# Turning the attention probabilities by DMA, as pairs of half floats

## What is computed

```python
q = rope(x @ wq.T + bq)      # 16 heads of 128
k = rope(x @ wk.T + bk)
v = x @ wv.T + bv
attn = einsum('bihd,bjhd->bhij', q, k) / sqrt(128)
attn = softmax(where(causal, -inf, attn))
o = einsum('bhij,bjhd->bihd', attn, v)
out = o @ wo.T + bo + residual
# beside it: 32 experts (top 4 of them for each token) and a shared expert
```

## Time and profile before

| | |
|---|---|
| median of 3 runs | 1025.46 us (1025.29 to 1025.47) |
| the profiled execution's own time | 1025.06 us |
| its span | 1023.3 us |
| PE busy | 1011.4 us, 99% |
| DVE busy | 711.6 us, 70% |
| ACT busy | 664.6 us, 65% |
| POOL busy | 774.1 us, 76% |
| granted TensorE clock | 1.00 of full speed over the span |

### The profile page before, as it was taken

One profiled execution on the slowest core, in us unless ns is written; L12 is line 12 of the kernel. 1 busy time (PEld: TensorE's weight loads), 2 busy tenths in 40 slices (PEclk: granted clock), 3 DMA queues, 4 the chain that ended last, 5 costly groups with the idle time before them and its releaser, 6 DMA issues.

```text
span 1023.3 us, 18770 instructions
## 1 busy us (share of the span) xinstructions
PE 1011.4 (99%) x6461; PEld 906.3 (89%) x6461; DVE 711.6 (70%) x1745; ACT 664.6 (65%) x1454; POOL 774.1 (76%) x660
## 2 busy tenths in 40 slices
PE   8999999999999999999999999999999999999998
PEld 4887898999989898989899899899998989898997
DVE  8757778787787888766666656666666566665676
ACT  5677666666667767665766656666566666656664
POOL 4879886758687786768786776978867879687866
PEclk9999999999999999999999999999999999999999
DMA  7222426212121212322232223333224232322232
GB/s 249 65 62 52 124 57 130 48 32 47 42 62 38 47 42 62 48 52 74 73 102 77 59 70 84 91 85 77 63 68 103 67 86 54 82 69 66 48 106 83
DMA packets 51694, 75.42 MB, mean 74 GB/s; under 512 B 12304, under 2 KB 29072, under 8 KB 51472
## 3 DMA queue, kind: packets, MB, share of 16 engines
q1 hardware_dynamic: 45920, 67.40, 25.2%
q0 software_dynamic: 5392, 6.56, 4.2%
q10 hardware_dynamic: 288, 0.26, 0.1%
HBM read 33.94 MB, written 10.90 MB: 44 GB/s over the span
## 4 chain that ended last, share of the span: by engine, by line
PE 93%; DVE 3%; POOL 1%; ACT 1%; DMA 1%; issue 0%; SPq 0%; DVEq 0%; POOLq 0%; ACTq 0%
PE ps L302 25%; PE ps L304 25%; PE ps L303 25%; PE ps L441 12%; PE ps L531 3%; PE ps L543 1%; DVE st L1238 1%; DVE ps L1552 0%; ACT prob L1044 0%; PE ps L517 0%; DMA xt<-x 0%; DVE xn L1264 0%; DVE acc L1599 0%; POOL qb L1705 0%; POOL qb L1701 0%
## 5 line engine op out<-in xcount | busy, mean ns | idle before, releaser
L1701 POOL TENSOR_TENSOR qb<-qb,k_sb 128x512 f32<-128x512 f32 x128 | 172.1, 1344 | 141.8 <-DMA qs<-qb 141.4
L1552 DVE CUSTOM_DVE_ANT_0 ps<-ps,maskr 128x128 f32<-128x128 f32 (+7 forms) x256 | 193.6, 762 | 57.4 <-PE ps L304 57.2
L1044 ACT ACTIVATE prob<-ps,nmax 128x128 f32<-128x128 f32 (+7 forms) x256 | 190.6, 744 | 60.7 <-DVE nmax L1552 59.1
L1055 ACT ACTIVATE ptd_h<-ps 128x128 fp32r<-128x128 f32 (+3 forms) x256 | 109.4, 436 | 147.3 <-PE ps L441 146.4
L1562 DVE TENSOR_TENSOR ptd_l<-ps,ptd_h 128x128 fp32r<-128x128 f32 (+3 forms) x256 | 124.4, 486 | 81.1 <-ACT ptd_h L1055 78.8
L1705 POOL TENSOR_TENSOR qb<-qb,qs 128x512 f32<-128x512 f32 x128 | 165.1, 1290 | 18.4
L441 PE MATMUL ps<-k_sb,prob 128*128 128x128 f32 x1152 | 172.7, 274 | 3.0 <-ACT prob L1044 1.5
L1702 POOL TENSOR_TENSOR qs<-qs,k_sb 128x512 f32<-128x512 f32 x128 | 172.5, 1348 | 0.0
L441 PEld LDWEIGHTS ps<-k_sb,prob 128*128 128x128 f32 x1152 | 135.2, 141 | 20.0 <-ACT prob L1044 2.6
L302 PE MATMUL ps<-k_h,q_h 128*128 128x512 f32 (+3 forms) x384 | 140.1, 365 | 0.0
L1599 DVE SCALAR_TENSOR_TENSOR acc<-ps,rinv,acc 128x256 f32<-128x256 f32 x256 | 111.4, 477 | 32.3 <-PE ps L304 30.8
(11 more groups left out here) (193 smaller groups left out, 2627.6 us busy)
## 6 DMA issues: line engine op xcount, KB each, us to landing
qs<-qb SPq DMA_DIRECT2D x256, 128.0 KB
ew<-epack SPq DMA_DIRECT2D x16, 768.0 KB, 4.2
rqk<-wqk SPq DMA_DIRECT2D x16, 256.0 KB, 3.0
rv<-wvp SPq DMA_DIRECT2D x8, 256.0 KB, 3.1
ro<-wop SPq DMA_DIRECT2D x16, 128.0 KB, 2.3
token_table<-xn SPq DMA_DIRECT2D x4, 512.0 KB, 5.1
token_sum<-token_table SPq DMA_DIRECT2D x1, 2048.0 KB, 9.3
token_sum<-x POOLq DMA_DIRECT2D x1, 2048.0 KB, 16.7
```

The source lines that it names most:

```text
L1044: act.activation(prob[:, t % 2, 0:w], tile[t], ACT.Exp, bias=nmax[:, t:t + 1], scale=-1.0, accum_out=rsum[:, t:t + 1]).then_inc(exp_done, 1)
L1055: act.activation(turned(0, t, j0, w), src, ACT.Copy).then_inc(pth_done, 1)
L1552: dve.tensor_tensor_reduce(out=tile[t], in0=tile[t], in1=maskr[:, SEQ - w:SEQ], scale=-1.0, scalar=3e38, op0=ALU.add, op1=ALU.min, accum_o ...
L1701: pool.tensor_tensor(qb[:, i, :], qb[:, i, :], cos_sb[:, c], ALU.mult).then_inc(rope_a, 1)
```

## The change

Transposes, and the copies out of PSUM behind them, go. `exps` writes the exponentials back into the tile's own place in PSUM. `prob_hi` on ACT scales them by 2^15 and writes them as a half float (float16) to `halves`, and `prob_lo` on DVE subtracts that from the scaled value and writes the rest as a second half float. `turn` is now a list entry of SP: for each tile two transposing DMAs (`dma_start_transpose`, the high and the low part, each of 128 x (t + 1) 128 elements of two bytes) from `halves` to `pt`, that is 16 DMAs in a unit. The four buffers of `halves` go by t mod 4, and `prob_hi` waits on `turned` of the tile four before it. `scores` waits on `lo_done` of the tile that was in its place, where it waited on `exp_done`.

`weighted` takes `pt` and the values, which are now split into half floats too, and has the same 36 matmuls. So that the values fit, `v_hi` and `v_lo` scale them by a power of two that the kernel works out for each pair of heads (`features`, `value_parts`, `value_scale` on DVE and `bound` on PE, once in four units), and `out_hi` and `out_lo` undo both scales (`oscale`).

```diff
-            def turn(n, g):
-                t, j0, w = TGROUPS[g]
-                pe.wait_ge(exp_done, TILES * n + t + 1)
-                bank = take("T", n, g)
-                for j in range(w):
-                    ins = pe.transpose(bank[:, j * P:(j + 1) * P], prob[:, t % 2, (j0 + j) * P:(j0 + j + 1) * P], ident)
-                ins.then_inc(t_done, 1)
...
-                    pe.wait_ge(exp_done, TILES * n + {0: -1, 2: 0, 4: 2, 5: 4, 6: 5, 7: 6}[t])
+                    pe.wait_ge(lo_done, TILES * n + {0: -1, 2: 0, 4: 2, 5: 4, 6: 5, 7: 6}[t])
...
+            def weighted(u, c):
+                for b in range(GT):
+                    pe.wait_ge(turned[b], 32 * (2 * u + c + 1))
+                pe.wait_ge(vl_done, 4 * (u // 2) + (2, 4)[c])
+                bank = take("PV", u, c)
+                d = slice(u % 2 * DK, (u % 2 + 1) * DK)
+                for j in range(4 * c + 4):
+                    a = max(0, j - 4 * c)
+                    ins = three(pe, bank[:, a * P:CH].rearrange("p (a b) -> p a b", b=P), (v_h[:, j, d], v_l[:, j, d]),
+                                [pt[c][i][:, a:GT, j, :] for i in range(2)], j == 0, j == 4 * c + 3)
...
+        def turn(sp, n, t):
+            if n and t % GT == 0:
+                sp.wait_ge(pv_done, 2 * (n - 1) + t // GT + 1)
+            for i, done in enumerate((hi_done, lo_done)):
+                sp.wait_ge(done, TILES * n + t + 1)
+                sp.dma_start_transpose(pt[t // GT][i][:, t % GT, 0:t + 1, :],
+                                       halves[t % GT][:, i, 0:(t + 1) * P]).then_inc(turned[t % GT], 16)
...
+                act.activation(tile[t], tile[t], ACT.Exp, bias=nmax[:, t:t + 1], scale=-1.0,
                                accum_out=rsum[:, t:t + 1]).then_inc(exp_done, 1)
...
+            def prob_hi(n, t):
+                act.wait_ge(exp_done, TILES * n + t + 1)
+                if n or t >= GT:
+                    act.wait_ge(turned[t % GT], 32 * (2 * n + t // GT))
+                act.activation(halves[t % GT][:, 0, 0:(t + 1) * P], tile[t], ACT.Copy, scale=PSCALE).then_inc(hi_done, 1)
...
+            def prob_lo(n, t):
+                dve.wait_ge(hi_done, TILES * n + t + 1)
+                h = halves[t % GT]
+                dve.scalar_tensor_tensor(out=h[:, 1, 0:(t + 1) * P], in0=tile[t], scalar=PSCALE, in1=h[:, 0, 0:(t + 1) * P],
+                                         op0=ALU.mult, op1=ALU.subtract).then_inc(lo_done, 1)
...
+            def value_parts(g):
+                scaled(dve.tensor_reduce(vpart[:, :], w, AX.X, ALU.max))
+                scaled(dve.tensor_reduce(vleast[:, :], w, AX.X, ALU.min))
+                scaled(dve.scalar_tensor_tensor(out=vpart[:, :], in0=vleast[:, :], scalar=-1.0, in1=vpart[:, :],
+                                                op0=ALU.mult, op1=ALU.max))
+                dve.tensor_tensor(vpart[:, :], vpart[:, :], xmax[:, :], ALU.mult).then_inc(vpart_done, 1)
```

More of the change, by code:

```diff
@@ L55 @@
 MASKS = 9
-TGROUPS = [(t, j, min(4, t + 1 - j)) for t in range(TILES) for j in range(0, t + 1, 4)]
-NTG = len(TGROUPS)
+PSCALE = 2.0 ** 15
+VTOP = 2.0 ** 14
 def batch_of(n):
@@ L478, in weighted_part @@
                 for j in range(last + 1):
-                    o = slice((2 * h + (j == last)) * P, (2 * h + 2) * P)
-                    if j < 4:
-                        pt = [ptr[i][:, j, o] for i in range(2)]
-                    else:
-                        pt = [ptd[i][:, j - 4, P + o.start:P + o.stop] for i in range(2)]
-                    ins = three(pe, bank[:, o], (v_h[:, j, d], v_l[:, j, d]), pt, j == 0, j == last)
+                    a = 2 * h + (j == last)
+                    ins = three(pe, bank[:, a * P:(2 * h + 2) * P].rearrange("p (a b) -> p a b", b=P),
+                                (v_h[:, j, d], v_l[:, j, d]), [pt[1][i][:, a:2 * h + 2, j, :] for i in range(2)],
+                                j == 0, j == last)
                 ins.then_inc(pv_done, 1)
@@ L586, in _ @@
             gate_turn(0)
+            bound(0)
             turn_x(2, 0)
@@ L674, in _ @@
                 masks(n, 3)
[L675 to L677 removed]
+                if n % 4 == 3:
+                    bound(n // 4 + 1)
+                weighted(n, 0)
             u = UNITS - 1
[L680 to L684 removed]
             outproj(u, 0, 0)
             outproj(u, 0, 1)
+            weighted_part(u, 0)
             weighted_part(u, 1)
@@ L780, in _ @@
                 g = n // 4
+                turn(sp, n - 1, 7)
                 load_ew(sp, n)
                 swap(sp, n + 1, 1)
+                for t in range(4):
+                    turn(sp, n, t)
                 swap(sp, n + 1, 2)
+                turn(sp, n, 4)
                 swap(sp, n + 1, 3)
+                turn(sp, n, 5)
                 if n == 1:
@@ L1065, in out_hi_part @@
                 o = slice(2 * h * P, (2 * h + 2) * P)
-                act.activation(oh[1][:, o], rbank("PW" if h else "PV", u, 1)[:, o], ACT.Copy).then_inc(oh_done, 1)
+                g = u // 4 % 2
+                act.activation(oh[1][:, o], rbank("PW" if h else "PV", u, 1)[:, o], ACT.Copy,
+                               scale=oscale[:, g:g + 1]).then_inc(oh_done, 1)
             def expert_tanh(n):
@@ L1330, in _ @@
             x_lo(1, 1)
+            dve.memset(sums[:, :], 1.0)
+            features()
+            value_parts(0)
             stats(2, 1)
@@ L1645, in _ @@
                 route(n, 0)
-                turned_lo(n, 1)
-                recips(n - 1, 1)
                 expert_copy(n)
-                turned_lo(n, 2)
+                prob_lo(n, 2)
+                prob_lo(n, 3)
                 recips(n, 0)
-                out_lo(n - 1, 1)
-                maxes(n, 4)
                 route(n, 1)
-                turned_lo(n, 3)
                 if n % 4 == 2 and g < PAIRS - 1:
@@ L1663, in _ @@
                     wo_lo(dve, 2 * g + 1)
+                maxes(n, 4)
+                if n % 4 == 3 and g < PAIRS - 1:
+                    value_parts(g + 1)
+                    wv_lo(dve, g + 1)
+                prob_lo(n, 4)
+                out_lo(n - 1, 1)
                 maxes(n, 5)
+                route(n, 2)
+                prob_lo(n, 5)
+                maxes(n, 6)
                 add_out(n - 1, 1, 0)
-                maxes(n, 6)
-                turned_lo(n, 4)
                 add_out(n - 1, 1, 1)
```

245 lines of the change are left out of this document (114 added, 131 removed).

## The result

The changed kernel takes 1084.02 us (median of 3 runs, 1083.92 to 1090.2) against 1025.46: ratio 1.059, interval 1.0535 to 1.0648. It is slower by 59 us, where the forecast of 918 us was faster by 107: a miss of 166 us, and outside the range. The median is one of three runs that lie 6.3 us apart, so that differences from it of that size are not clear of noise.

A forecast was written before the change was run, and what follows sets the result against it. PE, busy 99%, was taken as the bound. Savings of 15 x (4.7 - 1.4) and 16 x (4.7 - 0.7) us, with 6 added, took 107.5 off 1023.3; with 1.8 around the span, 918 us, range 880 to 1,035.

The forecast's parts named there:

- The waits this makes: Walk through two plain units' lists: PE loses 1.4 us a plain unit; 0.7 us taken with expert work.
- ACT and DVE: Same 36 blocks in 8 operations each in place of 12; some 17 us of 25 busy, costing latency, not throughput.
- POOL behind the swaps: POOL's waits for swaps queued behind turns on SP: 2.7 us of room in expert units, costed at nothing.
- the ring: Named after the run: mask, exponential, high, low, next mask; one tile at a time round DVE and ACT.
- POOL bound: Rival: swaps come 1 to 3 us later behind the turns, expert units go by POOL; 934 to 958 us, chance 0.07.
- The issue price: SP's time to issue a DMA, 0.47 or 0.60 us; sixteen make 8.5 us a unit, hidden.
- SP's cover: SP's issuing stays hidden in a 25 us unit until an issue takes 1.3 us.
- The rival on the slower side: Transposes' throughput: tiles go out in small pieces, PE waits at both weighted sums; 1,200 or 2,000 us, chance 0.20.
- The clock: PE's granted clock, taken as 1.00; a fall in PE's new gaps would show the forecast wrong.
- Tile 7's landing: Its turned low part lands 2.3 us after issue, covered by 0.6 us before weighted(n-1, 1), the thinnest cover.
- the swap loop: Named after the run: projection copy, swap's place in SP's list, landing, three POOL operations, `rope_hi` on ACT.
- C, the banks held longer: Theory of the experiments: a tile keeps its PSUM banks for four steps in place of two, and scores wait.

The follow-up runs named there:

- e1_merged: Changed kernel with one transposing DMA for both parts of a tile, 8 in a unit in place of 16, same bytes: 1106.0 us.
- e2_one_block: Changed kernel with the sixteen DMAs turning only the first block of each tile, which the weighted sum takes for all blocks: 1072.1 us.
- e18_early_ahead_late: Changed kernel with swap 2 behind turn 1, mask passes ahead of low parts (tiles 4 to 7), `rope_hi` behind high part 4: 1043.3 us.

## Why the prediction was wrong

**The step that failed** is "The waits this makes", with the sentence under ACT and DVE that leads to it: "Neither comes near its unit: some 17 us of 25. Here the change does not cost throughput, it costs latency." Its verdict is true: neither engine is full, and the cost is latency. Its size is not: DVE is busy 671.7 / 31 = 21.7 us a unit and ACT 18.9, where the earlier trace rows already had 20.7 and 18.6 in a plain unit. And I priced the latency only at the places of my walk, around tile 7 and at the unit's end, as 1.4 us and 0.7 us a unit, with nothing at tiles 4 to 6 and nothing for `rope_hi`. Measured, PE is idle for 4.5 us a unit and loses 1.8 more with it, 6.3 in all. I never followed the four steps of one tile into the mask of the next as a loop of its own. In unit 17 the four tiles' steps from mask 4 (612.29) to the exponential of tile 7 (629.21) take 17 us, in which DVE sits idle for 4.39 + 2.34 + 0.52 = 7.3 us and ACT for some 9.

**"POOL behind the swaps ... I cost them at nothing"** failed with it, and made it worse. POOL had the room that I gave it (22.7 us busy of 31), but its output stands in ACT's list ahead of high parts, so POOL's lateness is paid in the ring: ACT waited 66.9 us for it, where it waited 9.5. I asked whether POOL would be full, and not who waits for it. The rival "POOL bound" had swaps 1 to 3 us late; swap 2 left a median 7.1 us behind its copy, and swap 1, which left on time, landed 1.6 us later than before. With each loop in place, removing the other gives 2 or 3%; the sum over both is 100 us.

**The issue price.** 0.47 or 0.60 us was taken for an issue, 1.27 came. My own threshold of 1.3 us (SP's cover) was nearly reached: 16 x 1.27 + 4.3 = 24.6 us. It was not the bound, since the unit went to 31 us (e1_merged). But four tiles' turnings hold SP for 10 us in one piece, and that piece stood ahead of swap 2.

**The rival on the slower side** had the right sign and the wrong mechanism: its limit was 1.6 us an issue or 20 us of DMA engines, with PE waiting at the weighted sums. PE waited there 7.1 us in all. Its count of packets was right: the queue has 311,296 more, 311,296 / 32 = 9,728 a unit, near my 9,216, most of them under 512 bytes (323,600, before 12,304). Its price was wrong: such packets took far less than 0.090 us each (0.639 x 1082.2 x 16 less 0.252 x 1023.3 x 16 is 6,940 us of one engine for them, 0.022 us each). That makes 13.6 us of the 16 engines a unit, near the 11.5 I took, so the engines were not the wall; the blocks that e2_one_block leaves out were worth 12 us. The reason given for this rival, that no DMA in the trace moves an element to another partition, was wrong as it stands: the swaps do, by whole rows.

A transposing DMA of one to eight blocks holds SP for 1.26 us, and one of two to sixteen for 1.33. The Trainium skill, "VectorE: DVE Perf Modes", section The three transpose paths, gives 1309 ns for one block by DMA; as a price of each further block this case does not bear it out. By the prices above an engine moves 243 bytes in 0.022 us for the turns and 1,468 bytes in 0.090 us otherwise, 11 against 16 bytes a nanosecond. The Trainium skill, "Advanced Engine Details and Errata", section X-Bar Transpose (TRN2), calls transposing DMAs as fast as regular ones; here they run at two thirds of the rate.

**The clock.** The sum took 1.00. It was 0.97, and the prediction names that only as a sign of error. Windows over unit 12 of the changed kernel (columns as above) show what goes before:

```profile
448.90:452.90 4.00, 4.00 (x25) 2.89 (x24) 3.93 (x7) 0.00 (x0) 3.79 (x4) 1.00 0.30 57
452.90:456.90 4.00, 0.75 (x4) 0.27 (x2) 1.94 (x5) 2.58 (x5) 0.00 (x0) 0.89 0.48 92
456.90:460.90 4.00, 3.70 (x13) 3.42 (x14) 1.83 (x4) 2.14 (x4) 1.66 (x2) 0.50 1.01 143
460.90:464.90 4.00, 4.00 (x28) 4.00 (x28) 3.60 (x8) 0.82 (x2) 3.86 (x4) 0.75 0.72 142
```

PE is idle for 3.2 us of the second window. The clock falls at its end (0.89) from 2.4 to 1.2 GHz, stays there through the third (0.50) and comes back in the middle of the fourth (0.75): some 0.9 + 4 + 2 = 6.9 us at the lower level, most of them with PE busy. If the mean of 0.97 is the two levels mixed, 6% of the time, some 58 us, went at the lower one, and half of that, at most 29 us or 0.9 us a unit, is lost work. Here a wait of PE cost more than its length.

**What held.** PE's work: the transposes went, and half-float matmuls of 512 columns stand 0.215 us apart, as the timeline of PE shows:

```profile
610.54 0.38 PE L305 MATMUL ps<-pt_l,v_h 128*128 128x512 f16 x1
610.75 0.38 PE L306 MATMUL ps<-pt_h,v_l 128*128 128x512 f16 x1
610.97 0.38 PE L304 MATMUL ps<-pt_h,v_h 128*128 128x512 f16 x1
```

The prices of ACT and DVE were near: 1.02 and 1.22 us for 0.95 and 1.15. Tile 7's landing was in time. The start until the first marker takes 8.8 us more than before, where I had 2; no run separated that, and it stays open. The end takes 1.5 us more, where I had 1.

**What stays open.** Without both loops the unit still takes (965.72 - 98.76) / 31 = 28.0 us, where my prices of PE make 24.9; the other 3 us were not taken apart. Part of them are waits of PE for turned tiles, 24.7 us in 6 places, up to 11.7 us each, against 7.1 us in the changed kernel. C, the banks held longer, has no clean test. And the swap loop's price is not split between swap 2's place in SP's list (20 us in e18_early_ahead_late) and swap 1's landing; ACT's waits divide about evenly (29.7 us at projection 1, 31.2 at the other three).

## What to carry to other kernels

A change that takes work from a full engine and adds steps to idle ones has to be priced as a loop: follow one tile through its steps until the next tile may begin, with all that stands between them in each list, and take the largest such loop beside the busy sums. Look for a second loop that shares an engine's list with the first, because then each hides the other: removing one here gave 2 to 3%, removing both 9%, and the same edit of a queue's order gave nothing or 20 us. Keep what pays by itself: the half floats alone, without the turning by DMA, gave 1.9%.
